# Attention of a four-layer stack: the softmax taken row tile by row tile, with ScalarE doing a part of it in the first run

## What is computed

```python
q = (x @ Wq.T).reshape(B, T, H, Dh)      # k and v alike; T = 512
q, k = _apply_rope(q, cos, sin), _apply_rope(k, cos, sin)   # layer 0 only
scores = einsum('bthd,bshd->bhts', q, k) * scale            # scale = 128 ** -0.5
scores = where(tril, scores, -inf)
attn = softmax(scores, axis=-1)
y = einsum('bhts,bshd->bthd', attn, v)
return y.reshape(B, T, H * Dh) / 3.0 @ Wo.T                 # layer 3: biases, no / 3
```

## Time and profile before

| what | value |
|---|---|
| median of 3 runs | 1690.88 us (1686.76 to 1694.84) |
| the profiled execution | 1697.32 us, its span 1695.5 us |
| PE busy | 1545.7 us, 91% of the span |
| DVE busy | 1141.4 us, 67% |
| ACT busy | 924.6 us, 55% |
| POOL busy | 705.5 us, 42% |
| mean granted clock of PE | 0.969 of full speed |
| run 1, 27 to 236 us: PE, DVE, ACT, POOL busy | 188.07, 167.99, 109.94, 181.94 us |
| run 2, 382 to 574 us | 184.13, 150.53, 113.81, 53.91 us |
| run 3, 1125 to 1322 us | 183.36, 124.29, 114.68, 42.62 us |
| run 4, 1419 to 1614 us | 181.94, 122.95, 113.06, 42.62 us |

### The profile page before, as it was taken

One profiled execution on the slowest core, in us unless ns is written; L12 is line 12 of the kernel. 1 busy time (PEld: TensorE's weight loads), 2 busy tenths in 40 slices (PEclk: granted clock), 3 DMA queues, 4 the chain that ended last, 5 costly groups with the idle time before them and its releaser, 6 DMA issues. The chain is left out here.

```text
span 1695.5 us, 26065 instructions
## 1 busy us (share of the span) xinstructions
PE 1545.7 (91%) x8400; PEld 1215.6 (72%) x8400; DVE 1141.4 (67%) x2492; ACT 924.6 (55%) x2012; POOL 705.5 (42%) x686
## 2 busy tenths in 40 slices
PE   5989989969999898999989988979998997999898
PEld 4767779967787798555535546768886886888787
DVE  5888867557887667899889964436666444566633
ACT  5555556856565566666476532245655444565543
POOL 5999853324211234089649760022122222221222
PEclk9999999989999999999999999889999998999999
DMA  4212223111112121150050000011111112111111
GB/s 125 84 53 78 75 75 105 43 54 35 42 48 91 60 94 60 38 190 1 1 205 23 1 7 7 1 57 41 49 37 72 56 38 70 50 40 43 66 60 46
DMA packets 34334, 98.37 MB, mean 58 GB/s; under 512 B 6389, under 2 KB 11257, under 8 KB 32073
## 3 DMA queue, kind: packets, MB, share of 16 engines
q1 hardware_dynamic: 33064, 90.95, 16.1%
q0 software_dynamic: 1184, 6.37, 1.1%
HBM read 96.12 MB, written 1.18 MB: 57 GB/s over the span
## 5 line engine op out<-in xcount | busy, mean ns | idle before, releaser
L919 POOL TENSOR_TENSOR head_low<-head,head_high 128x512 fp32r<-128x512 f32 x64 | 81.8, 1278 | 464.6 <-ACT head_high L909 463.9
L1883 POOL TENSOR_TENSOR experts_low<-experts,experts_high 128x1536 fp32r<-128x1536 f32 (+3 forms) x56 | 126.6, 2261 | 250.3 <-ACT experts_high L1833 88.3
L1275 ACT ACTIVATE probs<-banks,neg_max 128x512 f32<-128x512 f32 (+3 forms) x256 | 131.4, 526 | 148.0 <-DVE neg_max L1183 148.0
L2428 POOL TENSOR_TENSOR rings<-du,bc_rows 128x512 f32<-128x512 f32 x124 | 155.3, 1271 | 21.1 <-DMA bc_rows<-bc_rows 14.3
L2354 DVE TENSOR_TENSOR_SCAN banks<-banks,rings 128x512 f32<-128x512 f32 x128 | 156.0, 1220 | 3.6 <-ACT banks L2252 2.2
L1525 DVE SCALAR_TENSOR_TENSOR hidden<-banks,weight,act_out 128x96 f32<-128x96 f32 (+1 forms) x192 | 62.7, 368 | 127.2 <-ACT act_out L1493 126.8
L2146 PE MATMUL banks<-rings,ident 128*128 128x512 f32 x256 | 127.8, 614 | 16.1 <-DVE rings L2377 15.8
L1493 ACT ACTIVATE act_out<-banks 128x256 f32<-128x256 f32 (+2 forms) x112 | 47.4, 423 | 171.9 <-PE banks L225 171.7
L225 PE MATMUL banks<-experts_high,xnT_high 128*128 128x384 f32 (+1 forms) x384 | 138.7, 361 | 0.5 <-PEq L187 0.5
L225 PE MATMUL banks<-xnT_high,head_high 128*128 128x512 f32 x256 | 109.9, 429 | 30.9 <-POOL head_low L919 25.0
L225 PE MATMUL banks<-experts_low,xnT_high 128*128 128x384 f32 (+1 forms) x384 | 137.1, 357 | 0.0
(11 more groups left out here) (302 smaller groups left out, 4709.1 us busy)
## 6 DMA issues: line engine op xcount, KB each, us to landing
head<-in_heads SPq DMA_DIRECT2D x64, 384.0 KB, 3.1
experts<-in_experts SPq DMA_DIRECT2D x16, 1152.0 KB, 5.2
bc_rows<-bc_rows SPq DMA_DIRECT2D x30, 512.0 KB, 5.9
experts<-in_experts SPq DMA_DIRECT2D x16, 768.0 KB, 4.2
values<-in_values SPq DMA_DIRECT2D x32, 256.0 KB, 3.2
coef<-in_spline_coef POOLq DMA_DIRECT2D x8, 768.0 KB, 4.6
idx<-in_lut_idx SPq DMA_DIRECT2D x16, 134.0 KB, 2.1
x<-in_x SPq DMA_DIRECT2D x2, 512.0 KB, 4.3
```

The costliest lines, as they stand in the source:

```text
L1275: last = nc.scalar.activation(prob_tile(i), score_tile(i), ACT.Exp, bias=neg_max[:, i:i + 1], scale=QK_SCALE, accum_out=row_sum[:, i:i + 1])
L1883: nc.gpsimd.tensor_tensor(parts[gpar][1][:, columns], raw[gpar][:, columns], parts[gpar][0][:, columns].bitcast(FP32), ALU.subtract)\
L2428: nc.gpsimd.tensor_tensor(inflow[:, step % INFLOWS], du[:, c], B_of(n), ALU.mult)\
```

## The change

The softmax is done in parts. The maxima are handed to ACT three times a head (tile 3; tile 2; tiles 1 and 0 together), so `max_ready` counts three a head. `exp_ready` counts two: behind tile 2 and behind tile 0. DVE takes the reciprocal and scales in two parts, tiles 3 and 2, then tiles 1 and 0. In the rotary runs `turn(h + 1, 0)` now stands between the two parts; before, it stood ahead of both.

In runs 2 to 4 DVE negates, in three instructions (128x1, 128x1, 128x2), each behind a wait for its own maximum. In run 1 (`spline`) ACT negates, with a copy that scales, and waits for its own result (`maxima_negated`) ahead of the exponential; and ACT also scales tile 3, the widest, behind the four exponentials (`scale_wide`), when DVE's reciprocal is there (`sums_inverted`). DVE then scales only tiles 2, 1 and 0, and PE waits for a second semaphore, `wide_ready`, ahead of the transposes.

```diff
--- before.py
+++ after.py
@@ -858,8 +858,10 @@
     exp_ready, probs_ready, v_ready = m.sig("exp_ready"), m.sig("probs_ready"), m.sig("v_ready")
     probsT_ready, y_ready, dve_chain = m.sig("probsT_ready"), m.sig("y_ready"), m.sig("dve_chain")
     rope_loaded, bias_loaded = m.sig("rope_loaded"), m.sig("bias_loaded")
+    negated = m.sig("maxima_negated")
+    inverted, wide_ready = m.sig("sums_inverted"), m.sig("wide_ready")
     CHAIN_QK = 5 if rotary else 0
-    CHAIN_SOFTMAX = 5
+    CHAIN_SOFTMAX = 2 if spline else 6
 
     if buffers is None:
         buffers = HeadBuffers(m, layer, ctx)
@@ -1092,6 +1094,8 @@
                 add_tiles(1 - par, (0, 1))
 
             pe.wait_ge(probs_ready.sem, probs_ready.at(h + 1))
+            if spline:
+                pe.wait_ge(wide_ready.sem, wide_ready.at(h + 1))
             turn()
             if not first:
                 add_tiles(1 - par, (2, 3)).then_inc(added.sem, 1)
@@ -1174,23 +1178,42 @@
                   .then_inc(v_low.sem, 1)
 
         def softmax(h, chain, next_turned=False):
+            def negate(tiles, last):
+                if spline:
+
+                    last.then_inc(max_ready.sem, 1)
+                    return
+                chain.link(last)
+                chain.wait()
+                nc.vector.tensor_scalar(neg_max[:, tiles], row_max[:, tiles], -QK_SCALE, None, ALU.mult)\
+                  .then_inc(max_ready.sem, 1)
+
+            def scale(n, tiles):
+
+                dve.wait_ge(exp_ready.sem, exp_ready.at(2 * h + n + 1))
+                inverse = nc.vector.reciprocal(row_inv[:, tiles], row_sum[:, tiles])
+                if spline and n == 0:
+                    inverse.then_inc(inverted.sem, 1)
+                    dve.wait_ge(inverted.sem, inverted.at(h + 1))
+                else:
+                    chain.all(inverse)
+                for i in (2,) if spline and n == 0 else (tiles.stop - 1, tiles.start):
+                    last = nc.vector.tensor_scalar(prob_tile(i), prob_tile(i), row_inv[:, i:i + 1], None, ALU.mult)
+                return last
+
             for n, i in enumerate((3, 2, 1, 0)):
                 if n < 3:
 
                     dve.wait_ge(scored.sem, scored.at(3 * h + n + 1))
-                chain.link(nc.vector.reduce_max(row_max[:, i:i + 1], score_tile(i), AXIS.X))
-            chain.wait()
-            nc.vector.tensor_scalar(neg_max[:], row_max[:], -QK_SCALE, None, ALU.mult)\
-              .then_inc(max_ready.sem, 1)
+                last = nc.vector.reduce_max(row_max[:, i:i + 1], score_tile(i), AXIS.X)
+                if i == 1:
+                    chain.link(last)
+                else:
+                    negate(slice(i, i + 1) if i else slice(0, 2), last)
+            scale(0, slice(2, 4))
             if next_turned:
                 turn(h + 1, 0, chain)
-
-            dve.wait_ge(exp_ready.sem, exp_ready.at(h + 1))
-            chain.all(nc.vector.reciprocal(row_inv[:], row_sum[:]))
-            for i in (3, 2, 1, 0):
-                last = nc.vector.tensor_scalar(prob_tile(i), prob_tile(i), row_inv[:, i:i + 1], None,
-                                               ALU.mult)
-            last.then_inc(probs_ready.sem, 1)
+            scale(1, slice(0, 2)).then_inc(probs_ready.sem, 1)
 
         def store_low(h):
 
@@ -1270,11 +1293,25 @@
 
         def exponentials(h):
 
-            act.wait_ge(max_ready.sem, max_ready.at(h + 1))
-            for i in (3, 2, 1, 0):
+            for n, i in enumerate((3, 2, 1, 0)):
+                if n < 3:
+
+                    act.wait_ge(max_ready.sem, max_ready.at(3 * h + n + 1))
+                    if spline:
+                        tiles = slice(i, i + 1) if n < 2 else slice(0, 2)
+                        nc.scalar.activation(neg_max[:, tiles], row_max[:, tiles], ACT.Copy, scale=-QK_SCALE)\
+                          .then_inc(negated.sem, 1)
+                        act.wait_ge(negated.sem, negated.at(3 * h + n + 1))
                 last = nc.scalar.activation(prob_tile(i), score_tile(i), ACT.Exp, bias=neg_max[:, i:i + 1],
                                             scale=QK_SCALE, accum_out=row_sum[:, i:i + 1])
-            last.then_inc(exp_ready.sem, 1)
+                if i in (2, 0):
+                    last.then_inc(exp_ready.sem, 1)
+
+        def scale_wide(h):
+
+            act.wait_ge(inverted.sem, inverted.at(h + 1))
+            nc.scalar.activation(prob_tile(3), prob_tile(3), ACT.Copy, scale=row_inv[:, 3:4])\
+              .then_inc(wide_ready.sem, 1)
 
         def store_turned(h):
             for k, (at, cols) in enumerate(TURNED_BANKS):
@@ -1303,6 +1340,8 @@
             par = c % 2
             last_heads = isinstance(h, int) and h >= HEADS - 2
             exponentials(h)
+            if spline:
+                scale_wide(h)
             spread_rest(h + 1)
             if not last_heads:
                 store_v(h + 2, par, (c // 2 + 1) % 2)
@@ -1327,6 +1366,8 @@
         if ahead:
             ahead.first_high(act)
         exponentials(HEADS - 1)
+        if spline:
+            scale_wide(HEADS - 1)
         if ahead and ahead.second_high:
             ahead.second_high(act)
         store_turned(HEADS - 1)
@@ -1358,7 +1399,7 @@
 
     def close():
         for s, n in ((qk_projected, 2 * HEADS), (v_projected, HEADS), (scored, 3 * HEADS), (turned, 3 * HEADS),
-                     (attended, HEADS), (added, HEADS + 1), (qk_ready, HEADS), (max_ready, HEADS), (exp_ready, HEADS),
+                     (attended, HEADS), (added, HEADS + 1), (qk_ready, HEADS), (max_ready, 3 * HEADS), (exp_ready, 2 * HEADS),
                      (probs_ready, HEADS), (v_ready, HEADS), (probsT_ready, 3 * HEADS), (y_ready, HEADS),
                      (dve_chain, HEADS * (CHAIN_QK + CHAIN_SOFTMAX))):
             s.close(n)
@@ -1367,6 +1408,10 @@
         for s in (values_high, values_split):
             s.close(PAIRS)
         rope_loaded.close(32)
+        if spline:
+            negated.close(3 * HEADS)
+            inverted.close(HEADS)
+            wide_ready.close(HEADS)
         if rotary:
             qk_rest_ready.close(HEADS)
         else:
```

## The result

The changed kernel takes 1679.42 us (median of 8 runs, 1675.88 to 1680.23) against 1692.36 us for the kernel before on the same chip: ratio 0.992, 95% interval 0.9907 to 0.9933, 12.9 us or 0.8% less. A second measurement gave 1678.18 us against 1693.28 us, ratio 0.9914 (0.9888 to 0.994). The forecast was 1672 us, 18.8 us less.

A forecast was written before the change was run, and what follows sets the result against it. PE, busy 91% of the span, was taken as the bound, its waits for scaled probabilities as the gain: 9.7 + 1.3 + 3.9 + 3.9 = 18.8 us for runs 1 to 4, from the median 1690.9 to 1672 us; range 1664 to 1684.

The forecast's parts named there:

- Run 1, 9.7 us: Attention run 1: 7 us from 13 heads at 0.55 us each, plus 1.2 and 1.5 us in heads 14 and 15.
- I leave 0.9 to 1.0 us of waits in each head: Run 1, DVE: waits for POOL that remain in each head after the change, 0.9 to 1.0 us.
- Rival A: Run 1: POOL's lock on tile 1's scaling lengthens waits 0.55 us, the 13 heads give nothing; 1679 us, chance 0.16.
- The floor by POOL: Run 1: POOL can give back only 0.6 us a head plus 2.8 us once, so 13 heads gain at most 10.6 us.
- Three exposed table loads: Run 1, heads 0, 4 and 8: ACT's 1.28 us table load comes behind the negation and takes the early start's gain.
- Run 2, +1.3 us: Run 2: heads 0 and 14 give 1.0 us, the last head 0.3 us, between a loss of 1 and gain of 2.
- Last heads of runs 3 and 4, 1.5 us: Last head of each: first negations held by POOL, tiles 3 and 2 scaled early, last scalings no longer caught; 1.5 us gained.
- Heads 0 and 14: 1.6 us saved: Runs 3 and 4: of 1.8 us these two heads wait together for probabilities, 1.6 us saved in each run.
- Value path, 0.8 us a run: Runs 3 and 4, steady heads: ACT's copy after the value product starts 0.06 us earlier, 0.8 us a run.
- Rival B: Run 1: tiles 2 and 1 both meet whole POOL additions, 4.0 us of waits a head; slower, 1712 us, chance 0.05.
- Rival D: Run 1 turns on a POOL, PE, ACT loop that earlier transposes don't shorten; only 5 us gained, 1686 us, chance 0.12.
- C: Last heads give nothing or lose, through POOL's 2.4 us pieces between the three negations; 1677 us, chance 0.07.

The follow-up runs named there:

- parts_run1_only: The changed softmax kept in attention run 1 only, runs 2 to 4 with the old one: 1682.82 us, ratio 0.9941 against the kernel before.
- run1_less_pool_work: The changed kernel with the spline rows leaving out the last term of the third row of widths, less work for POOL: 1677.21 us, ratio 0.9908.
- before_again: The kernel before, unedited, profiled a second time: 1690.97 us.
- parts_runs2to4_only: The old softmax in attention run 1, the one in parts in runs 2 to 4: 1691.26 us, ratio 0.9987 against the kernel before.
- run1_dve_negates: The changed kernel, but in attention run 1 DVE negates the maxima while ACT still scales tile 3: 1677.43 us, ratio 0.991.
- after_again: The changed kernel, unedited, profiled a second time: 1678.18 us.

## Why the prediction was right, and where not

The time lies in the range and on the right side, 7 us above the forecast. By steps, with the ledger's runs:

- *Run 1, 9.7 us*: about 12 (208.6 and 209.2 against 196.0 and 197.4), 10 by the medians of parts_run1_only. The 0.55 us a head held: a pair is 1.14 us shorter, and heads 1 to 13 gave 8.3 to 8.6 us together where 7 were said. Head 0 gave 0.7 us that the sum did not have, head 15 0.2 to 0.7 us and not 1.5. Head 14 gave 2.6 us (14.13 to 11.49) and not 1.2: PE's wait fell by 1.0 us (2.19 to 1.17), and the rest is the granted clock. It fell to half behind the longer wait in all three profiles with the old softmax in run 1, and stays full in head 14 of the changed kernel. The sum has no term for the clock, so in that head the fit is luck. Window of PE in before:

```profile
216.00:218.00 2.00, 2.00 (x5) 0.50 0.00 0
```

  PE's wait of 9.9 us stood in the window of 9 to 12, two heads at 24.65 in 24.6 to 24.9. POOL's wait for ACT fell from 9.2 to 3.0 us, which is not near zero. The exponential of tile 3 starts 0.27 us behind its maximum (0.35 said). ACT's scaling took 0.72 us (0.69 taken).
- *"I leave 0.9 to 1.0 us of waits in each head"*: it is more, and uneven: 0.6 us in even heads (tile 1), where it costs PE nothing, 2.2 us in odd ones (1.09 less 0.47 at tile 2, 2.10 less 0.55 at tiles 1 and 0). On the mean that is 1.4 us a head, just under the 1.5 us that was to prove the forecast wrong. Rival A's remark that the phase repeats every two heads was the right picture.
- *The floor by POOL*: the number fits by coincidence. POOL's whole work doesn't bind (run1_less_pool_work); what sets the pace in its place is argued above, not shown.
- *Three exposed table loads*: wrong but for a rest. The load runs ahead of the copy and not behind it. In head 0 it is over before the maximum is there; in heads 4 and 8 it ends late, and the first exponential comes 1.21 us behind the start of the maxima, not 0.95. Timeline of ACT at the first two passes of run 1's loop:

```profile
27.08 1.28 ACT L1302 ACT_TABLE_LOAD   x1
29.58 0.20 ACT L1302 ACTIVATE neg_max<-row_max 128x1 f32<-128x1 f32 x1 [1.22 <-DVE row_max L1208]
...
76.00 1.28 ACT L1302 ACT_TABLE_LOAD   x1
77.29 0.20 ACT L1302 ACTIVATE neg_max<-row_max 128x1 f32<-128x1 f32 x1
```

By the Trainium skill's 2.66 us a switch ("ScalarE: Activation LUTs", "What ACT_TABLE_LOAD costs") run 1 would have given 5.6 us; it gave 10 to 12. At the second pass the negation starts 1.29 us after the load does, so no drain of 1.38 us shows.
- *Run 2, +1.3 us*: the step that failed most. It lost some 2 us: 190.7 to 192.4 us in the six profiles with the new softmax and nothing held, 189.1 to 190.4 in the three with the old one. Head 14 gave 0.36 us less waiting and head 0 0.3 us, but in the last head "a loss of 1" was exceeded: 2.46 us more of waiting, in all six. The scalings are split in time, and each half meets a piece of POOL's work.
- *Last heads of runs 3 and 4, 1.5 us*: 1.2 each (5.37 to 4.15 and 4.23). The size is near, by luck, for the way was wrong at each step. The one-column negations, said to be held, took 0.15 us beside POOL. Tile 3's scaling, said to be done in the gap, was caught (1.39 us). And "it no longer catches a scaling" failed, by 2.73 us for tiles 1 and 0 (DVE, then POOL):

```profile
1581.63 0.15 DVE L1188 TENSOR_SCALAR neg_max<-row_max 128x1 f32<-128x1 f32 x1
...
1583.00 0.92 DVE L1188 TENSOR_SCALAR neg_max<-row_max 128x2 f32<-128x2 f32 x1
...
1585.85 2.73 DVE L1201 TENSOR_SCALAR probs<-probs,row_inv 128x256 f32<-128x256 f32 x2
```

```profile
1585.90 2.34 POOL L1928 TENSOR_TENSOR experts_low<-experts,experts_high 128x1024 fp32r<-128x1024 f32 x1 [0.76 <-ACT experts_high L1871]
```

  POOL's third subtraction waits for a copy that ACT makes behind the exponentials. With no negation held ahead of the first two, the exponentials ended at 1584.87, 2.4 us earlier in the head than reckoned, and the subtraction came forward with them. DVE's second half could have begun then too, but stood behind tile 3's held scaling (to 1585.41) and tile 2's. So the first catch moves the second scaling onto the next subtraction, and the two start within 0.05 us. The prediction's "whoever comes first" can't be read off start times so close: here tile 1's scaling starts first and takes 2.53 us, while in run 3 of the same profile it starts first by as much (1295.45, POOL at 1295.50), takes 0.35 us, and tile 0's behind it is the one that is held. PE waits 4.15 to 4.23 us either way.
- *"Heads 0 and 14: 1.6 us saved"* in each of runs 3 and 4: head 14 gave about 1.4, head 0 0.1 us at most, and in 14 of 20 cases the clock fell behind it. That the next wait of head 0, for the transposed tiles, would take the gain was in no term.
- *Value path, 0.8 us a run*: 1.2 to 1.5 us between heads 1 and 14 where the clock didn't fall, some 0.1 us a head against 0.06 said.
- *Against the median*: the offset of 6.4 us was carried over rightly, and before_again shows that it was chance. Runs 2 to 4 were to give 9.1 us and gave 2 by parts_runs2to4_only. That is the whole miss of 6 to 7 us. The range's upper end is a little wide: the middle between A (1679) and D (1686) is 1682.5 us, not 1684.

Rival B's mechanism, two requests that both meet POOL, is real in odd heads, at 2.2 us where B had 4.0, and in run 2's last head. Rival D is refuted by run 1's 10 us. The measured 1679.4 us is A's number, but not A's mechanism, since run 1 gave its whole gain; C had the right place, the last heads, with the wrong instructions.

## What to carry to other kernels

Cutting one step into two doubles the moments at which it can be caught by another engine's long instructions. List for each half what the other engine starts at that time and what releases it, remember that such work moves forward with your own, and hold back what nobody needs yet. Removing a wait is worth only what the next wait in the same head doesn't take, so read that row too. Weigh small changes by the stages that were edited and by many runs, since the unedited stages here ranged over 13 us from profile to profile.

## What was not expected of the hardware

- A DVE operation of one column, 128x1, is not held by POOL's long instructions: no negation of one column took over 0.16 us in any kernel here, though some fifty began inside an instruction of POOL of over 1 us. The same of two columns, 128x2, is held (2.50 and 0.92 us in last heads, 1.41 us beside additions in run1_dve_negates). A reciprocal of 128x2 isn't (0.17 us at 105.51 and 117.68, inside additions).
- DVE's rotary multiplications, one of whose operands lies in PSUM, ran at 0.68 us each inside an addition of POOL's (104.80, addition from 104.42 to 106.27), as they do outside one.
- Of a DVE and a POOL instruction that start within 0.05 us of each other, the earlier one by the trace's times was held in some cases and not in others (2.53 us at 1585.85, 0.35 us at 1295.45).
- A single pause of PE of 1.67 us behind ten transposes was followed by half clock in some executions and not in others of the same kernel, after and after_again.
